# Attention read-out plus a dense layer on one core: the last four tiles of a transposed by TensorE, and three products moved into the seventh step

## The reference, cut to what matters

```python
xn = layernorm(x)                                   # x: (8, 256, 512), 2048 rows
q = (xn @ Wq.T + bq).reshape(b, s, 32, 128)
sig_q = elu(q) + 1
q_sel = sig_q[:, :, ::4, :]                         # 8 heads of 128
num = einsum('bshd,hde->bshe', q_sel, M)
den = einsum('bshd,hd->bsh', q_sel, z)[..., None] + 1e-6
out_heads = repeat(num / den, 4, axis=2)
attn = out_heads.reshape(b, s, 4096) @ Wo.T
ffn = xn @ (w.astype(float32) * w_scale) + b        # w: int8, 512 x 512
return x + attn + ffn
```

## Time and profile before

| | |
|---|---|
| median of 3 runs | 269.68 us (269.05 to 270.76) |
| the profiled execution, its own time | 271.09 us |
| its span, from first to last instruction | 269.4 us |
| PE busy | 245.0 us, 91% of the span |
| DVE busy | 176.4 us, 65% |
| ACT busy | 119.8 us, 44% |
| POOL busy | 106.0 us, 39% |
| granted TensorE clock, mean over the span | 0.968 |
| chain that ended last, by engine | PE 61%, SP's queue 18%, DVE 10% |

### The profile page before, as it was taken

One profiled execution on the slowest core, in us unless ns is written; L12 is line 12 of the kernel. 1 busy time (PEld: TensorE's weight loads), 2 busy tenths in 40 slices (PEclk: granted clock), 3 DMA queues, 4 the chain that ended last, 5 costly groups with the idle time before them and its releaser, 6 DMA issues.

```text
span 269.4 us, 3377 instructions
## 1 busy us (share of the span) xinstructions
PE 245.0 (91%) x1030; PEld 191.5 (71%) x1030; DVE 176.4 (65%) x261; ACT 119.8 (44%) x276; POOL 106.0 (39%) x97
## 2 busy tenths in 40 slices
PE   7899898999979999999999999999999996295665
PEld 2487686877728888888888888888888875174465
DVE  3849968997897499594949595858476954132021
ACT  3743816575478244636363544445347505101010
POOL 2694455561508153616161625250508880000000
PEclk9999999999999999999999999999999999868968
DMA  7999999992702114234251522212121222222141
GB/s 254 411 415 401 317 225 212 207 212 74 238 0 52 49 50 122 70 103 150 56 157 50 156 64 72 71 45 73 49 73 49 88 53 83 88 53 81 49 160 39
DMA packets 22097, 34.83 MB, mean 129 GB/s; under 512 B 5184, under 2 KB 13632, under 8 KB 20928
## 3 DMA queue, kind: packets, MB, share of 16 engines
q1 hardware_dynamic: 20928, 27.81, 31.8%
q0 software_dynamic: 864, 6.29, 11.4%
q10 hardware_dynamic: 288, 0.52, 0.5%
HBM read 22.02 MB, written 4.19 MB: 97 GB/s over the span
## 4 chain that ended last, share of the span: by engine, by line
PE 61%; SPq 18%; DVE 10%; issue 4%; ACT 3%; DMA 2%; DVEq 0%
SPq L200 18%; PE q_ps L734 9%; PE q_ps L736 9%; PE q_ps L735 8%; PE attn_ps L734 7%; PE attn_ps L736 7%; PE attn_ps L735 7%; PE dense_ps L734 4%; PE dense_ps L736 4%; PE dense_ps L735 4%; PE attn_ps L797 2%; DVE stats L510 1%; DMA x<-in_x 1%; DVE wd_lo L565 1%; DVE s L586 1%
## 5 line engine op out<-in xcount | busy, mean ns | idle before, releaser
L734 PE MATMUL attn_ps<-P_hi,aT_hi 128*128 128x512 f32 (+1 forms) x128 | 53.4, 417 | 14.8 <-DVE aT_lo L612 14.8
L298 POOL TENSOR_TENSOR e_and_sz<-s,z_b 128x512 f32<-128x512 f32 x32 | 42.8, 1367 | 43.1 <-DVE den L591 43.0
L422 ACT ACTIVATE s<-s,rden 128x128 f32<-128x128 f32 x128 | 39.2, 389 | 39.4 <-DVE rden L595 39.4
L735 PE MATMUL attn_ps<-P_lo,aT_hi 128*128 128x512 f32 (+1 forms) x128 | 52.2, 408 | 0.0
L736 PE MATMUL attn_ps<-P_hi,aT_lo 128*128 128x512 f32 (+1 forms) x128 | 52.0, 406 | 0.0
L734 PE MATMUL q_ps<-WqT_hi,xT_hi 128*128 128x512 f32 x104 | 41.8, 402 | 0.9 <-DVE s L586 0.6
L734 PEld LDWEIGHTS attn_ps<-P_hi,aT_hi 128*128 128x128 f32 x128 | 25.9, 203 | 22.4 <-issue 11.7
L736 PE MATMUL q_ps<-WqT_hi,xT_lo 128*128 128x512 f32 x104 | 40.6, 390 | 0.0
L735 PE MATMUL q_ps<-WqT_lo,xT_hi 128*128 128x512 f32 x104 | 40.5, 390 | 0.0
L579 DVE SCALAR_TENSOR_TENSOR q_ps<-q_ps,rstd,bq_b 128x512 f32<-128x512 f32 x28 | 21.1, 756 | 24.5 <-PE q_ps L736 24.4
L268 POOL TENSOR_TENSOR xT<-xT,mean_b 128x512 f32<-128x512 f32 x14 | 19.9, 1424 | 34.8 <-ACT mean_b L371 32.4
(11 more groups left out here) (80 smaller groups left out, 368.2 us busy)
## 6 DMA issues: line engine op xcount, KB each, us to landing
x<-in_WoT POOLq DMA_DIRECT2D x6, 1024.0 KB, 10.0
x<-in_x SPq DMA_DIRECT2D x16, 256.0 KB, 4.7
xT<-in_xT SPq DMA_DIRECT2D x16, 256.0 KB, 5.0
aT<-s SPq DMA_DIRECT2D x128, 32.0 KB, 1.8
MT<-s SPq DMA_DIRECT2D x128, 32.0 KB, 1.9
out<-x SPq DMA_DIRECT2D x15, 256.0 KB, 2.3
x<-in_WoT SPq DMA_DIRECT2D x2, 1024.0 KB, 14.1
s<-in_WqT SPq DMA_DIRECT2D x3, 512.0 KB, 6.7
```

The source lines that it names most:

```text
L298: nc.gpsimd.tensor_tensor(sz_eps[:, :, h * D // 2:(h + 1) * D // 2].rearrange("p g (j c) -> p j g c", j=2), by_quarter(sbuf_s[:, t % SRING ...
L422: last = nc.scalar.activation(a_g, a_g, ACT.Copy, scale=rden[:, t % 2, g:g + 1])
L734: nc.tensor.matmul(out, x_hi, w_hi, start=start, stop=False)
L735: nc.tensor.matmul(out, x_hi, w_lo, start=False, stop=False)
```

## The change

Four things change.

1. Tiles 12 to 15 (`FIRST_BY_PE` and up) are no longer block-turned by DVE and moved by SP. `make_a` writes their a head by head into the memory of `xT`, which is free by then, and PE transposes it there, eight transposes of 128x128 per tile, into two of the four q banks (`turn_a`). ACT and DVE make the high and the low part out of those banks. The transposes stand on PE behind the read-outs of tiles 8, 9, 11 and 12.
2. The denominators and a of the last tiles are made earlier: step 14 now does tiles 11 and 12 and step 15 tiles 13 and 14, and only tile 15 comes after the loop.
3. P(5), P(6) and P(7) are made inside step 7, between the pieces of q(7) and dense(7), with their high and low parts. The moments of tile 8 and the low part of xT(7) come earlier on DVE.
4. Which place takes which tile changes: tile 1 now goes to `aT` (and waits for tile 0's parts), even tiles from 2 on to the memory of `MT`, which need P made; odd ones to `aT`. Also, `add_dense(2)` stands ahead of `denominator(0)` on DVE.

```diff
+    FIRST_BY_PE = T - 4
+        def denominators_of_step(t):
+            return {T - 2: [T - 5, T - 4], T - 1: [T - 3, T - 2]}.get(t, [t - BEHIND])
+        def in_MT(t):
+            return t >= 2 and t % 2 == 0
...
+        def a_by_head(t, g):
+            return xT[:, 2 * (t % 2):2 * (t % 2) + 2, :, :].rearrange("p r k c -> p (r k c)")[:, g * D:(g + 1) * D]
+
+        def turned_ps(t, h):
+            return q_ps[2 * (t % 2) + h]
...
             def spread_blocks(t):
                 sp.wait_ge(a_turned, t + 1)
                 if t == 1:
+                    sp.wait_ge(aT_lo_ready, 2)
+                elif t == 2:
                     sp.wait_ge(P_filled, G)
-                elif t >= 2:
+                elif t >= 3:
                     sp.wait_ge(aT_lo_ready, 2 * t - 2)
...
-            for t in range(T - BEHIND - 1, T):
-                spread_blocks(t)
-                store(t - BEHIND - 1)
-            for t in range(T - BEHIND - 1, T - 1):
+            for t in range(T - LEAD - 1, T - 1):
                 store(t)
...
             def make_a(t):
                 act.wait_ge(rden_ready, t + 1)
                 act.wait_ge(sz_ready, 2 * t + 2)
+                if FIRST_BY_PE <= t < FIRST_BY_PE + 2:
+                    act.wait_ge(xT_lo_ready, T + 1)
+                elif t >= FIRST_BY_PE + 2:
+                    act.wait_ge(turned_by_pe, 2 * (t - FIRST_BY_PE - 1))
...
             def copy_aT_hi(t):
...
+                        act.wait_ge(turned_by_pe, 2 * (t - FIRST_BY_PE) + h + 1)
+                        nc.scalar.activation(aT_hi[:, t % 2, gs, :].rearrange("p g r -> p (g r)"), turned_ps(t, h)[:], ACT.Copy
+                                             ).then_inc(aT_hi_ready, 1)
...
-            copy_P_hi(5)
-            copy_P_hi(6)
             make_a(2)
-            copy_P_hi(7)
             copy_mean(8)
             make_a(3)
             for t in range(LEAD, T):
+                if t == LEAD:
+                    copy_P_hi(5)
                 exp_of(t, 0)
                 if t + 1 < T:
                     copy_xT_hi(t + 1)
+                if t == LEAD:
+                    copy_P_hi(6)
                 exp_of(t, 1)
+                if t == LEAD:
+                    copy_P_hi(7)
                 copy_aT_hi(t - LEAD + 1)
...
+                    else:
+                        nc.vector.tensor_tensor(aT_lo[:, t % 2, gs, :].rearrange("p g r -> p (g r)"), turned_ps(t, h)[:],
+                                                aT_hi[:, t % 2, gs, :].rearrange("p g r -> p (g r)").bitcast(F32),
+                                                ALU.subtract).then_inc(aT_lo_ready, 1)
...
+            def turn_a(t):
+                pe.wait_ge(a_ready, t + 1)
+                for h in range(2):
+                    if t < T - 2:
+                        pe.wait_ge(s_ready, 2 * (t + 2) + h + 1)
+                    else:
+                        pe.wait_ge(aT_lo_ready, 2 * (t - 2) + h + 1)
+                    for i in range(GH):
+                        last = nc.tensor.transpose(turned_ps(t, h)[:, i * P:(i + 1) * P],
+                                                   a_by_head(t, h * GH + i), ident[:])
+                    last.then_inc(turned_by_pe, 1)
...
-            product_P(5)
-            product_P(6)
-            product_P(7)
             spread_mean(8)
             for t in range(LEAD, T):
                 product_q(t, 0)
+                if t == LEAD:
+                    product_P(5)
                 product_q(t, 1)
-                product_dense(t)
+                if t == LEAD:
+                    product_P(6)
+                product_dense(t, 0, K // 2)
+                if t == LEAD:
+                    product_P(7)
+                product_dense(t, K // 2, K)
                 if t + 2 < T:
                     spread_mean(t + 2)
                 product_attn(t - LEAD)
+            turn_a(FIRST_BY_PE)
             for t in range(T - LEAD, T - 1):
                 product_attn(t)
+                if t == T - LEAD:
+                    turn_a(FIRST_BY_PE + 1)
+                elif T - LEAD + 2 <= t < T - LEAD + 4:
+                    turn_a(t + 3)
```

More of the change, by code:

```diff
@@ L169, in aT_landed @@
         def aT_landed(t):
-            return 16 * 16 * (t // 2 + 1)
+            return 16 * 16 * sum(in_MT(u) == in_MT(t) for u in range(t + 1))
+        def a_by_head(t, g):
+            return xT[:, 2 * (t % 2):2 * (t % 2) + 2, :, :].rearrange("p r k c -> p (r k c)")[:, g * D:(g + 1) * D]
+        def turned_ps(t, h):
+            return q_ps[2 * (t % 2) + h]
         def chunks(j):
@@ L351, in _ @@
             for t in range(LEAD, T):
-                times_z(t - BEHIND, 0)
-                times_z(t - BEHIND, 1)
+                for u in denominators_of_step(t):
+                    times_z(u, 0)
+                    times_z(u, 1)
                 add_b(t - LEAD + 1)
@@ L357, in _ @@
                     center(t + 2)
[L358 to L362, removed]
+            times_z(T - 1, 0)
+            times_z(T - 1, 1)
+            add_b(T - LEAD + 1)
+            for t in range(T - LEAD + 2, T):
                 add_b(t)
@@ L497, in _ @@
                     copy_mean(t + 2)
-                make_a(t - BEHIND)
-            for t in range(T - LEAD + 1, T):
+                for u in denominators_of_step(t):
+                    if u < T - 2:
+                        make_a(u)
+            copy_aT_hi(T - LEAD + 1)
+            make_a(T - 2)
+            copy_aT_hi(T - LEAD + 2)
+            make_a(T - 1)
+            for t in range(FIRST_BY_PE, T):
                 copy_aT_hi(t)
-                if t + BEHIND < T:
-                    make_a(t + BEHIND)
         @block.vector
@@ L712, in _ @@
                 add_dense(t)
-                denominator(t - BEHIND)
-                if t == T - 1:
-                    denominator(T - BEHIND)
+                for u in denominators_of_step(t):
+                    denominator(u)
                 add_attn(t - LEAD)
@@ L718, in _ @@
                 split_aT_lo(t + 1)
[L719 to L722, removed]
+                if t == T - LEAD:
+                    denominator(T - 1)
                 add_attn(t)
@@ L777, in product_q, with product_dense @@
                 last.then_inc(q_filled, 1)
-            def product_dense(t):
-                if t >= 1:
+            def product_dense(t, first=0, end=K):
+                if t >= 1 and first == 0:
                     pe.wait_ge(dense_added, t)
-                for k in range(K):
+                for k in range(first, end):
                     if t == 0:
@@ L786, in product_dense @@
                                         wd_hi[:, k, :], wd_lo[:, k, :], k == 0, k == K - 1)
-                last.then_inc(dense_filled, 1)
+                if end == K:
+                    last.then_inc(dense_filled, 1)
             def product_P(g):
```

42 lines of the change are left out of this document (26 added, 16 removed).

## The result

The changed kernel takes 249.66 us (median of 4 runs, 249.36 to 250.26) against 269.44 us (4 runs, 269.05 to 270.76) for the kernel before on the same chip: a ratio of 0.926, 95% interval 0.922 to 0.930. Forecast were 248.8 us and a range of 247.2 to 253.0. The profiled execution's own time is 249.62 us, its span 247.8 us, against 271.09 and 269.4.

A forecast was written before the change was run, and what follows sets the result against it. SP's issuing of moves was taken to bound the tail. From the profiled 271.09 us, minus 22.2, 1.1 and 1.1, plus 3.5, gave 250.2; the same 20.9 off 269.68 gave 248.8 us, range 247.2 to 253.0.

The forecast's parts named there:

- The bound of the tail: Kernel's end: read-outs wait 14.8 us for low parts of aT, because SP needs 10 us of issuing per tile.
- The 22.2 us: Tail: time lost to waits (14.8), around them (0.6) and the low clock (6.7), all taken as won back.
- The transposes: Tail, on PE: 32 of 128x128 added in line with the read-outs, 0.11 us each, 3.5 us in all.
- dense(3): Front: PE no longer waits for the addition of dense(2); 1.1 us won, bounds 0 and 1.3.
- P(5) to P(7): Front, step 7: 2.6 us idle removed, new 1.5 us wait before read-out 0; net 1.1 us won, bounds 0 and 2.6.
- Tile 1 into `aT`: Front: its moves wait for tile 0's low parts instead of P(7); no cost, no gain.
- The slacks of the tail: Tail: every a and low part is ready before PE asks, shortest slack 2 us for tile 11; no wait left.
- Dear transposes: Rival, tail: transposes cost 0.17 to 0.27 us each, giving 250.7 to 254.0 us; chance 0.13.
- a front without gain: Rival, front: ACT's a(2) and a(3) push out the low part of P(7), giving 249.9 to 251.0 us; chance 0.13.
- a new wait in the tail: Rival, tail: likeliest the chain denominator 13, POOL, denominator 14; costs 1 to 3 us, 250 to 252; chance 0.08.
- falls of the clock: Rival, tail: waits or transposes let the clock fall one to three times, 2 us each, 250.8 to 255; chance 0.08.
- The slow case: Rival, tail: transposes keep the clock low from tile 9 on, 33 us more, 281 us; chance 0.02.

The follow-up runs named there:

- throw-away matmuls: The kernel before, with throw-away bf16 matmuls behind the read-outs of tiles 11 to 14 to fill the gaps: 268.40 us, ratio 0.995.
- the front alone: The changed kernel with all 16 tiles through block turns and moves and the last denominators and a in their former order: 267.30 us, ratio 0.988.
- the old places: The changed kernel with odd tiles in the memory of MT again, so tile 1's moves wait for P(7): 257.96 us, ratio 0.954.
- the fourfold transposes: The changed kernel with each of the 32 transposes done four times, 128 in all: 260.52 us, ratio 0.967.
- the kernel with two queues: The kernel before, with eight of the 16 moves of each of tiles 12 to 15 issued by ACT instead of SP: 261.90 us, ratio 0.971.

## Why the prediction was right, step by step

**The bound of the tail: right.** SP's issuing set the end, shown from both sides: by taking the moves away and by sharing them out.

**The 22.2 us: right by the trace, too large by the runs.** In the profile the first read-out ran at 85.82 and the last matmul ended at 245.06. From there on before took 266.5 - 88.7 = 177.8 us, after 159.2: 18.6 saved, against 22.2 - 3.5 = 18.7 forecast. But the sum was made against one execution of 271.09 us, slower than each of the four timed runs, and taken over to the median unchanged. That is the term that was off: spans differ by 21.6 us, medians by 19.8. What makes an execution of the kernel before longer or shorter is at least in part how much of the last read-out falls on the low clock: throw-away matmuls won 2.8 us in the profiled span and 1.2 in the runs. The profiled execution had nearly all of that loss. The single executions bear this out: of the 17 of the kernel before beside that run, seven had a mean granted clock of 0.968 and took 270.2 us on average, ten had 0.974 or 0.975 and took 269.4; of the eleven on another chip, five at 0.968 took 270.7 and six at 0.974 or 0.975 took 269.8. Where the difference lies the front alone shows, whose profiled execution was one of 0.974. Its last read-out starts at 254.72 and is back at the full pitch after 3.8 us; the one of the kernel before starts at 257.99 and is back after 6.3 (the first matmuls at full pitch, in this order):

```profile
258.47 0.28 PE L773 MATMUL attn_ps<-P_hi,aT_hi 128*128 128x256 f32 x1
```
```profile
264.28 0.28 PE L736 MATMUL q_ps<-P_hi,aT_lo 128*128 128x256 f32 x1
```

What makes the clock come back sooner or later from one execution to the next is not shown.

**The transposes: right**, 3.5 us forecast, 0.87 us for eight measured. The pitch of one transpose among matmuls held for eight in a row; the length of its record, 0.27 us, would have given 8.6.

**dense(3): right**, 1.1 us forecast, 1.2 measured by putting it back.

**P(5) to P(7): right in kind, short in size.** 1.1 us forecast; with dense(3) the front gave 2.85 and not 2.2. The new wait was 0.84 us with a late start of 1.0 in all, not 1.5: my walk through the queues of ACT and DVE had the low part of P(7) 0.6 us too late.

**Tile 1 into `aT`: right.** Its moves began at 77.09, the low part of xT(8) was there at 90.3 (90.8 forecast), and q(8) asked for it at 91.53. "No gain" holds for this part by itself only: with P(7) made later, the old places cost 7.7 us.

**The slacks of the tail: right.** a(12) was ready at 193.7 and used at 202.3 (195 and 202.8 forecast), a(13) at 203.0 and 208.8, a(14) at 206.8 and 220.8, a(15) at 213.3 and 227.3. The shortest, for tile 11, was 1.6 us where 2 were forecast: low parts at 213.6, read-out at 215.2. The prediction gave no price for the earlier denominators; the trace gives 0.7 us, which the runs do not tell from nothing.

**The rivals.** Dear transposes, a front without gain, a new wait in the tail, falls of the clock: none came. The slow case with its clock is out by the fourfold transposes. One measure was too generous: the prediction took only gaps of 2.7 us and more for those that bring the clock down, and in the kernel with two queues 2.15 us did. It did no harm, since the tail had no idle at all.

## What to carry to other kernels

If the end of a kernel waits for a queue that only issues, count its issues: 16 small DMAs at 0.63 us are 10 us, and here a store of 256 KB kept SP no longer (0.58) than a move of 32 KB. An engine that is nearly the bound can still be the cheaper place, here 0.87 us on PE against 10.0 of issuing on SP. Price a wait of PE with the clock behind it, 2 us for ten matmuls, and price a saving against the median execution, not against the one that was profiled. When work is moved into a busy step, look at who waited for its last piece.

## What was not expected of the hardware

- Groups of 32 transposes, 3.66 us each, left the granted clock at 1.00.
- A wait of 2.2 us behind 0.87 us of transposes brought the clock down (0.60 in the next 4 us). The transposes are not needed for that: in the kernel with two queues waits of 2.15 and 2.26 us right behind read-outs did so too (a record of 0.63 us is one at the lower level). One of 2.77 us in the kernel before did not and one of 2.78 did, and one of 2.84 in the front alone did not. The length of the idle alone does not tell.

```profile
218.57 0.65 PE L745 MATMUL attn_ps<-P_hi,aT_hi 128*128 128x512 f32 x1 [2.15 <-DVE aT_lo L623]
...
228.20 0.47 PE L745 MATMUL attn_ps<-P_hi,aT_hi 128*128 128x512 f32 x1 [2.26 <-DVE aT_lo L623]
...
229.00 0.63 PE L745 MATMUL attn_ps<-P_hi,aT_hi 128*128 128x512 f32 x1
```

- DVE's low parts of aT, 1.27 us for the pair, took 2.91 and 3.17 us where POOL was at work on z or b at the same time, in the tail of the changed kernel:

```profile
197.15 1.27 DVE L644 TENSOR_TENSOR aT_lo<-aT,aT_hi 128x512 fp32r<-128x512 f32 x2
...
204.82 2.91 DVE L644 TENSOR_TENSOR aT_lo<-MT,aT_hi 128x512 fp32r<-128x512 f32 x2
...
210.45 3.17 DVE L644 TENSOR_TENSOR aT_lo<-aT,aT_hi 128x512 fp32r<-128x512 f32 x2 [0.78 <-ACT aT_hi L451]
```

The pairs out of PSUM, from 216.05 on, took 1.29 us each, but POOL had just ended its work then. The kernel before has both cases with the same operands, out of SBUF: a pair during POOL's work (212.88 to 221.35), and one behind it:

```profile
213.53 2.91 DVE L612 TENSOR_TENSOR aT_lo<-MT,aT_hi 128x512 fp32r<-128x512 f32 x2
...
223.97 1.29 DVE L612 TENSOR_TENSOR aT_lo<-aT,aT_hi 128x512 fp32r<-128x512 f32 x2 [4.47 <-ACT aT_hi L431]
```

No run was made in which POOL's work was moved, so that the cause is argued from the times alone.
